# A GNN layer pair on one core: x is written back in superblock order during the first edge stage and read from there in the second merge

## What is computed

```
msg = x[src] @ W_msg + edge_attr @ W_edge
agg = segment_max(msg, dst, num_segments=N); agg = where(isneginf(agg), 0, agg)
conv = agg + x @ W_root + b
c1 = leaky_relu(conv(X,  layer 1 weights))
c2 = leaky_relu(conv(c1, layer 2 weights))
out = layernorm(X + c2, axis=-1)          # eps 1e-5
```

## Time and profile before

| | us |
|---|---|
| median of 3 runs | 2060.19 (2059.29 to 2060.62) |
| the profiled execution | 2056.28 |
| its span in the trace | 2054.5 |
| PE / DVE / ACT / POOL busy in the span | 1648.0 / 1329.4 / 1085.5 / 1219.3 |
| moved by DMA | 440.17 MB, 214 GB/s on average |

### The profile page before, as it was taken

The page is one execution under the profiler, slowest core; times in us unless marked ns, Lnnn a source line. Parts: engine busy times, 40 slices in busy tenths (PEclk is TensorE's granted clock), DMA queues, the critical chain, the costliest instruction groups (busy, mean ns, idle before and its releaser), DMA issues.

```text
span 2054.5 us, 38144 instructions
## 1 busy us (share of the span) xinstructions
PE 1648.0 (80%) x11634; PEld 1385.5 (67%) x11634; DVE 1329.4 (65%) x2435; ACT 1085.5 (53%) x2452; POOL 1219.3 (59%) x1307
## 2 busy tenths in 40 slices
PE   4899999999876777766699999999987766656553
PEld 2378888888766666666477777778776665556552
DVE  4375555555544444444377777777728999999997
ACT  1144444444223334434366666666627777777776
POOL 7777777777244444444577777777747555545432
PEclk9799999999999999999899999999999988898976
DMA  4377878787545666666477777777758888888885
GB/s 70 73 195 223 235 220 236 218 235 221 183 154 204 212 226 231 238 244 233 155 209 214 207 210 213 209 204 222 205 195 251 255 258 260 263 263 266 261 259 141
DMA packets 537287, 440.17 MB, mean 214 GB/s; under 512 B 444819, under 2 KB 446170, under 8 KB 537098
## 3 DMA queue, kind: packets, MB, share of 16 engines
q1 hardware_dynamic: 469324, 282.86, 47.6%
q0 software_dynamic: 38032, 77.00, 13.8%
q10 hardware_dynamic: 29742, 77.88, 10.1%
HBM read 264.25 MB, written 173.37 MB: 213 GB/s over the span
## 4 chain that ended last, share of the span: by engine, by line
PE 42%; DVE 25%; POOL 18%; issue 12%; DMA 2%; ACT 1%; SPq 1%; DVEq 0%; POOLq 0%; ACTq 0%
POOL arena L359 16%; PE ps L537 15%; PE ps L456 10%; DVE stats L923 6%; PE ps L447 5%; DVE arena L921 5%; PE ps L427 4%; DVE arena L918 4%; DVE onehot L903 4%; PE ps L416 2%; PE ps L421 2%; PE ps L435 2%; DMA arena<-nodes,src_perm 1%; DVE small L934 1%; DVE small L930 1%
## 5 line engine op out<-in xcount | busy, mean ns | idle before, releaser
L537 PE MATMUL ps<-hold,onehot 128*128 x4688 | 651.3, 300 | 309.0 <-POOL onehot L404 154.1
L537 PEld LDWEIGHTS ps<-hold,onehot 128*128 128x128 f32 x4688 | 604.9, 210 | 356.7 <-issue 356.1
L359 POOL DMA_INDIRECT arena<-in_x_dram,src_all x392 | 377.6, 963 | 135.4 <-issue 115.7
L456 PEld LDWEIGHTS ps<-w_root,onehot 97*128 97x128 f32 x3136 | 395.5, 192 | 91.3 <-issue 90.9
L359 POOL DMA_INDIRECT arena<-nodes,src_perm x392 | 370.1, 944 | 126.4 <-issue 123.6
L456 PE MATMUL ps<-w_root,onehot 97*128 97x128 f32 x3136 | 413.6, 275 | 0.0
L843 DVE TENSOR_TENSOR_SCAN arena<-keep,arena,ps 96x512 f32<-96x512 bf16 x196 | 248.5, 1268 | 168.5 <-PE ps L427 167.8
L903 DVE TENSOR_TENSOR onehot<-count,rel 128x1024 f32<-128x1024 bf16 x147 | 188.9, 1285 | 257.2 <-PE ps L537 206.2
L657 ACT COPY arena<-ps 128x384 f32<-128x384 f32 x392 | 166.3, 475 | 314.7 <-PE ps L537 314.7
L404 POOL CAST onehot<-keep 128x1024 f32<-128x1024 uint8 x147 | 197.2, 1342 | 201.1 <-ACT ps L643 160.3
L375 POOL CAST arena<-onehot 128x1024 uint8<-128x1024 f32 x147 | 153.9, 1047 | 256.7 <-DVE onehot L903 256.6
(11 more groups left out here) (105 smaller groups left out, 1578.2 us busy)
## 6 DMA issues: line engine op xcount, KB each, us to landing
root<-arena ACTq DMA_DIRECT2D x196, 384.0 KB
arena<-root SPq DMA_DIRECT2D x196, 384.0 KB, 5.2
nodes<-arena SPq DMA_DIRECT2D x49, 768.0 KB, 4.1
arena<-nodes SPq DMA_DIRECT2D x98, 384.0 KB
arena<-in_x_dram SPq DMA_DIRECT2D x97, 384.0 KB
arena<-in_x_dram SPq DMA_DIRECT2D x48, 768.0 KB, 7.1
out_dram<-arena SPq DMA_DIRECT2D x48, 768.0 KB, 4.9
keep<-onehot_bytes POOLq DMA_DIRECT2D x147, 128.0 KB, 4.1
```

Source lines behind the costliest of these rows:

```text
L359: nc.gpsimd.indirect_dma_start(out=gathered[t.ring][0:t.p, i, 0:D], out_offset=None, in_=table_in, in_offset=bass.IndirectOffsetOnAxis(ap= ...
L456: last = nc.tensor.matmul(no_ps[m % 2][:, i * P:(i + 1) * P], nodes_t[m % NODE_RING][0:D + 1, i * P:(i + 1) * P], w_root[0:D + 1, layer * ...
L537: nc.tensor.matmul(ps[:, bass.ds(place_at, P)], onehot[:, k % NS, i, :], flat[:, bass.ds(chunks[i % WORDS], P)], start=False, stop=True, s ...
```

## The change

A new table `x_again` in superblock order. In the edge stage of layer 0, SP stores every unit of x that it has loaded, out of the same buffer `node_in`, to `x_again` (one store of 384 KB, 128 runs of 3072 bytes). The store of unit u waits for its load (`block_in`). The next load into that buffer waits for the store (`x_kept`), beside the old wait. The last stage's `load_x` reads from `x_again`: one transfer of 128 runs of 6144 bytes in the place of 2048 runs of 384 bytes.

```
+            def keep_x(u):
+                tail = 1 if u == NU - 1 and U_END % P else 0
+                sp.wait_ge(block_in[u % UNIT_RING], DMA * (u // UNIT_RING + 1 + tail))
+                sp.dma_start(unit_of(x_again, u), node_in[u % UNIT_RING]).then_inc(x_kept[u % UNIT_RING], DMA)
...
 load_nodes:
+                if u >= UNIT_RING and not layer:
+                    sp.wait_ge(x_kept[u % UNIT_RING], DMA * (u // UNIT_RING))
...
 edge_phase, in group g between the keep row and the x loads, and after the last group:
+                    while layer == 0 and (kept_x + 1) * UG <= node_groups(0, max(g - 2, 0)).stop:
+                        keep_x(kept_x)
+                        kept_x += 1
...
+                while layer == 0 and kept_x < NU:
+                    keep_x(kept_x)
+                    kept_x += 1
...
 load_x:
-                rows = N_END if s == NSB - 1 else SBN
-                full = rows // P
-                to = x_in[s % 2].rearrange("p (j d) -> p j d", d=D)
-                at = x[s * SBN:s * SBN + full * P, :].rearrange("(j p) d -> p j d", p=P)
-                sp.dma_start(to[:, 0:full, :], at).then_inc(x_back[s % 2], DMA)
-                if rows > full * P:
-                    sp.dma_start(to[0:rows - full * P, full, :], x[s * SBN + full * P:N, :]).then_inc(x_back[s % 2], DMA)
+                sp.dma_start(x_in[s % 2], table(x_again, s)).then_inc(x_back[s % 2], DMA)
...
 before the release of layer 1's gathers:
+            for i in range(UNIT_RING):
+                sp.wait_ge(x_kept[i], DMA * ((NU + UNIT_RING - 1 - i) // UNIT_RING))
...
 finish(s) on DVE:
-                tail = 1 if s == NSB - 1 and N_END % P else 0
-                dve.wait_ge(x_back[s % 2], DMA * (s // 2 + 1 + tail))
+                dve.wait_ge(x_back[s % 2], DMA * (s // 2 + 1))
```

More of the change, by code:

```diff
@@ L79, in gnn @@
         nodes_1 = nc.dram_tensor("nodes_1", (NSB * SBN, D), F32, kind="Internal").ap()
+        x_again = nc.dram_tensor("x_again", (NSB * SBN, D), F32, kind="Internal").ap()
         keep_dram = nc.dram_tensor("keep_row", (E,), BF16, kind="Internal").ap()
@@ L171, in gnn @@
             "ones_set", "turned", "scaled", "et_done", "em_full", "scanned", "eb_full", "held"))
+        x_kept = sems("x_kept", UNIT_RING)
         block_in, nt_full, nt_scaled, nt_done = sems("block_in", UNIT_RING), sem("nt_full"), sem("nt_scaled"), sem("nt_done")
@@ L253, in load_nodes @@
                     sp.dma_start(to[0:rows - full * P, full, :], x[u * UN + full * P:N, :]).then_inc(block_in[u % UNIT_RING], DMA)
+            def keep_x(u):
+                tail = 1 if u == NU - 1 and U_END % P else 0
+                sp.wait_ge(block_in[u % UNIT_RING], DMA * (u // UNIT_RING + 1 + tail))
+                sp.dma_start(unit_of(x_again, u), node_in[u % UNIT_RING]).then_inc(x_kept[u % UNIT_RING], DMA)
             def edge_phase(layer):
+                kept_x = 0
                 for g in range(NE):
```

## The result

The changed kernel takes 2079.52 us in the median of 6 runs (2073.01 to 2085.86), the kernel before 2059.02 in 6 (2057.43 to 2060.62): a ratio of 1.0097, 95% interval 1.0076 to 1.0117, or some 20 us slower. The profiled execution took 2075.59 us with a span of 2073.8, 19.3 more than the 2054.5 before.

What follows compares the result with a forecast made beforehand. Stage 4 was taken as bound by a chain of DVE instructions, stage 1 by PE, busy throughout. Terms 0 + 0 + 2 + 0 = +2 us on the profiled 2056.3, plus 3.9 to the median, gave 2062.2; range 2055 to 2090.

Steps and rivals of the forecast that it cites:

- the absorbed case: Whole kernel: the added stores and waits cost almost nothing, 2058 to 2066 us; chance 0.48.
- the rival of late x units: Stage 1: x loads land late behind the load, store, load order on SP; some +12 us, 2074; chance 0.17.
- Part 1, stage 4: Stage 4: x loads in long rows get cheaper, but nobody waits for them; 0 us, bound -6.2 us.
- Part 2, bytes: Stage 1: the DMA engines have room for 98 more stores, at share 1.00 and 308 GB/s; 0 us.
- The rival of full DMA engines: Stage 1: the DMA engines become the bound; +22 us at a ceiling of 0.95, up to +64; chance 0.26.
- Part 3, the waits on SP: Stage 1: SP waits 0.4 us in the median for a unit's load; +2 us allowed for single late units.
- Part 3, the room of 2.9 us: Stage 1: an x load needs 6.6 of the 9.5 us before PE turns its unit, leaving 2.9 us.
- Part 3, the reserve: Stage 1: new issues take 0.4 us a group of the 3.6 us that SP spends waiting for PE.
- The signs: Right: stage 1 PE busy throughout, DMA share near 1.0; wrong: PE waiting for x units, stage 1 ending after 545 us.
- the shorter x add: Stage 4: the x add on DVE gets faster without short x rows; 23.6 us less, 2037; chance 0.04.
- The start of stage 4: Start of stage 4: the first two x loads hold SP for less time; -6.2 us, 2054 to 2056; chance 0.05.
- Part 4: The ends of stage 1's stores and waits, with stages 2 and 3 untouched: 0 us.

Runs made afterwards that it cites:

- f1_bytes: Changed kernel storing the same bytes from a zeroed area, without both new waits, stage 4 reading x as before: 1.0000 against the kernel before at 2058.98 us.
- f2_waits: Changed kernel with all stores and both waits but an eighth of the bytes, stage 4 reading x from the input: 1.0003 against the kernel before at 2058.98 us.
- h2_load_wait: Full bytes stored from a zeroed area, plus only SP's wait for the unit's load: 2088.82 us, 1.0150 against the kernel before at 2059.43 us.
- e4_long: Kernel before with only stage 4's x load replaced by long rows from nodes_1: 1.0007 against the kernel before at 2274 us.

## Why the prediction came out as it did

The range held, and the chances leaned to no side: slower had 0.45, the same 0.46. But the forecast of 2062, the absorbed case, was not what happened; what happened is of the kind of the rival of late x units, with 0.17. That 2079.5 lies in the range is luck: its upper end, 2090, was there for the ceiling of the DMA engines, which f1_bytes refutes. It is luck as well that 2079.5 is near the rival's 2074. By its own terms, a third of 93 units at 1.0 us each, the rival costs 31 us and not 12, which gives 2093. Its condition, a landing of 10.5 us, didn't come true either: the slowest took 9.8.

- **Part 1, stage 4**: right in the sum, 0 us, and for the reason given. Wrong in one detail: the issue of an x load was to fall from 1519 ns to some 400 and is 1516, with runs of 6144 bytes. The issue time there is not set by the load's own rows alone. The first two loads did shrink, from 7.00 to 1.14 us, and gave nothing back, as said. The landing got shorter by 0.4 of 7.1 us, not by a fifth.
- **Part 2, bytes**: right. 308 GB/s and a share of 1.00 were forecast; f1_bytes shows 311 and 1.01 at no cost. The rival of full DMA engines, 0.26, is refuted: the bursts of the earlier trace rows were the better guide to what a stretch can hold than stage 4's 0.87.
- **Part 3, the waits on SP**: this is the step that failed. I put SP's wait behind a load one group old at 5.2 - 4.8 = 0.4 us in the median. It was 93.3 us in 50 waits, 1.9 us each, and both terms were off. The landing time came from `root` loads, of stages 2 and 4 at shares of 0.61 and 0.84, and was used for x loads at 1.00. By the semaphore events of the traces, an x load (83 of them, from unit 14 on) landed in 3.9 us in the median before, 4.0 in f2_waits, 5.9 in f1_bytes and 6.1 in the changed kernel. And the load was younger than a group: at the 45 stores with one keep row between load and store, SP asked 3.9 us after the issue in the median, at the least 1.7, and the loads landed after 5.8. Keep rows lie 4.8 us apart only as long as SP is early and waits for PE at each; once it is late, it comes to the store as soon as the issues between are done.
- **Part 3, the room of 2.9 us**: an x load was to have 9.5 us until PE turns the unit. Before, the least from unit 4 on was 9.1; the ten units that PE waited for had between 5.5 and 7.6. One wait of 2.9 us ahead of the load, as in the place shown, takes all of that room.
- **Part 3, the reserve**: the 3.6 us a group that SP had free were counted against 0.4 us of new issues. The attributes' issue grew from 595 to 1044 ns in the median with the higher load, a term that the sum doesn't have, and SP's wait at the keep row sank from 287.9 to 81.0 us. With the bytes alone it was 112.9, with the waits alone 227.2. The two costs fall in one in-order stream and add up; the sum of Part 3 had the first at 0.4 us a group and the second at 0.4.
- **The signs**: of those named, the DMA share, DVE's times and the lower share in stage 4 (0.80) came as said. SP's waits of 1.9 us, PE's waits for x units and the end of stage 1 after 545 us were the signs of being wrong.
- **The granted clock** has no term in the prediction; its falls behind PE's waits are an estimated 3.4 of the 17.4 us.
- **The other rivals**: the shorter x add is refuted (2473 ns before and after). The start of stage 4 gained nothing.
- **Part 4**: 0 was said for stages 2 and 3, which came out 1.9 us longer in one execution. The stores and the wait don't do it by themselves: f1_bytes has 961.1 us there and h2_load_wait 961.2, against 961.5 before. The cause is open.
- **Two slips without effect**: 131 MB at 325 GB/s are 403 us, not 402. And POOL, called nearly as full as PE in stage 1, is busy 299.40 of the 425 us.

## What to carry to other kernels

Bytes and waits can each be free and costly together: here 38.5 MB more cost nothing, two waits more cost nothing, and the first wait with the bytes cost 1.5%. Price a wait for a DMA with the landing time at the load that will be there, not with one from another stage, and with the age that the load will have once the issuing engine is late. Count what stands behind the wait in its in-order queue: a load held back by a few us is the next one to be waited for. And a cheaper transfer is worth only what someone waited for it, which in stage 4 was 0 us.

## What the runs showed of the hardware

- Sixteen engines held a packet share of 1.01 and 311 GB/s over 425 us, with x rows of 384 bytes and stores mixed, and the matrix engine lost nothing. The Trainium skill, "DMA: Bandwidth & Descriptors", Specifications, gives about 358 GB/s for one core's share of the HBM; no long stretch here reached that, and a burst of 2 us did 404, above it.
- The time to issue a DMA on SP grows with the load on the DMA engines: the attributes' DMA takes 595 ns in the median at a share of 0.78 (before), 602 at 0.85 (f2_waits), 1044 at 0.99 (changed kernel) and 1532 at 1.01 (f1_bytes). The landing time of the 384 KB x load is 3.9 and 4.0 us in the first two and 6.1 and 5.9 in the last two.
- The clock granted to PE fell to its lower level, 1.2 GHz, behind six idle times of PE of 1.6 to 3.3 us (two in the changed kernel, four in h2_load_wait), in a stretch where the kernel before has it at the upper level throughout. Behind one of 1.85 us it stayed up. In one such place the eight matmuls of L468 took 1.91 us in the place of 1.06.
- One and the same kernel took 2059 us on some chips and 2260 to 2275 on others, with longer waits between engines. In e4_long, whose stage 1 is unchanged, single instructions are nearly the same as in the kernel before: 948 and 945 ns for a gather's issue, 286 and 275 for a matmul of L456 (L450 there). A change that fills slack can cost 1% on the one and 0.2% or nothing on the other.
